# A fused four-layer attention and expert kernel: the scores of two heads are computed together at every second step, the turn of the probabilities stands behind q's product, and the output products at the step's end

## The reference, cut to what matters

```python
x = x + jnp.tanh(g_xattn[0]) * _L0_xattn_ref(_layernorm(x), ctx_2048, ...)   # 16 heads of 128
x = x + jnp.tanh(g_ffn[0])   * _L0_ffn_ref(_layernorm(x), ...)               # 8 experts, the best 2
x = x + jnp.tanh(g_xattn[1]) * _L1_xattn_ref(_layernorm(x), ctx_2048, ctx_2048)
x = x + jnp.tanh(g_ffn[1])   * _L1_ffn_ref(_layernorm(x), ...)               # 8 experts, the best 1
# first layer, for each sequence b and head h:
q = rms_norm(x @ q_w + q_b, nq_s);  k = rms_norm(ctx @ ki_w + ki_b, nki_s);  v = ctx @ vi_w + vi_b
scores = jnp.einsum('bshd,blhd->bhsl', q, k) * scale
attn = softmax(scores);  out = jnp.einsum('bhsl,blhd->bshd', attn, v);  out @ o_w + o_b
```

## Time and profile before

| | |
|---|---|
| median of the runs | 1361.11 us |
| the profiled execution | 1362.31 us, its span 1360.5 us |
| TensorE: matmuls | 1332.2 us busy, 98% |
| TensorE: weight loads | 1170.8 us busy, 86% |
| VectorE / ScalarE | 769.0 us (57%) / 761.0 us (56%) |
| GpSimd | 74.1 us (5%) |
| granted TensorE clock, mean | 0.997 |

### The profile page before, as it was taken

One profiled execution on the slowest core, in us unless ns is written; L12 is line 12 of the kernel. 1 busy time (PEld: TensorE's weight loads), 2 busy tenths in 40 slices (PEclk: granted clock), 3 DMA queues, 4 the chain that ended last, 5 costly groups with the idle time before them and its releaser, 6 DMA issues.

```text
span 1360.5 us, 26830 instructions
## 1 busy us (share of the span) xinstructions
PE 1332.2 (98%) x10479; PEld 1170.8 (86%) x10479; DVE 769.0 (57%) x2323; ACT 761.0 (56%) x2084; POOL 74.1 (5%) x114
## 2 busy tenths in 40 slices
PE   7899999999999999999999999999999999999998
PEld 6788888988898888988889888998889888888877
DVE  7644556546565464664555465564656555554575
ACT  4375666566465564756556564555646556456522
POOL 3000000010000000000000100001000000001010
PEclk9999999999999999999999999999999999999999
DMA  8312522223122321222212231122312112122100
GB/s 300 112 63 78 140 94 74 68 66 121 47 78 64 94 94 47 63 94 83 89 47 77 69 120 63 47 79 92 111 32 78 63 63 94 49 76 72 54 1 32
DMA packets 51452, 108.48 MB, mean 80 GB/s; under 512 B 8224, under 2 KB 32000, under 8 KB 50688
## 3 DMA queue, kind: packets, MB, share of 16 engines
q1 hardware_dynamic: 51328, 106.77, 24.2%
HBM read 89.98 MB, written 16.78 MB: 78 GB/s over the span
## 4 chain that ended last, share of the span: by engine, by line
PE 86%; DVE 10%; ACT 3%; issue 1%; DMA 0%; SPq 0%; DVEq 0%
PE bank L114 57%; PE bank L1044 8%; PE bank L1054 5%; PE bank L1015 3%; PE bank L1033 3%; PE bank L1154 2%; PE bank L1166 2%; PE bank L1191 1%; PE bank L1005 1%; PE bank L1108 1%; ACT xn L783 1%; PE bank L985 1%; DVE rstd L80 1%; DVE logit L1516 1%; DVE ao_lo L1507 1%
## 5 line engine op out<-in xcount | busy, mean ns | idle before, releaser
L114 PE MATMUL bank<-sv,ct_hi 128*128 128x256 f32 x1024 | 195.4, 289 | 0.0
L114 PE MATMUL bank<-so,ao_hi 128*128 128x256 f32 x1016 | 187.6, 284 | 0.3 <-DVE ao_lo L1507 0.3
L1507 DVE SCALAR_TENSOR_TENSOR ao_lo<-bank,vecs,ao_hi 128x512 fp32r<-128x512 f32 x127 | 95.3, 751 | 159.6 <-ACT ao_hi L752 158.4
L758 ACT ACTIVATE expo<-logit,least 128x64 f32<-128x64 f32 x512 | 171.6, 337 | 21.7 <-DVE least L1518 21.7
L752 ACT ACTIVATE ao_hi<-bank,vecs 128x512 fp32r<-128x512 f32 x127 | 87.0, 685 | 154.4 <-PE bank L1044 153.8
L114 PEld LDWEIGHTS bank<-so,ao_hi 128*128 128x128 f32 x1016 | 162.1, 189 | 8.5 <-issue 0.5
L114 PEld LDWEIGHTS bank<-sv,ct_hi 128*128 128x128 f32 x1024 | 156.3, 189 | 0.1
L777 ACT ACTIVATE q_sb<-bank,qbias,qscale 128x512 f32<-128x512 f32 x128 | 99.3, 776 | 87.2 <-PE bank L114 86.7
L1516 DVE TENSOR_TENSOR logit<-bank,rr 128x256 f32<-128x256 f32 x128 | 54.3, 424 | 163.3 <-PE bank L1054 162.7
L114 PE MATMUL bank<-sv,ct_lo 128*128 128x256 f32 x512 | 143.2, 280 | 0.0
L114 PE MATMUL bank<-so,ao_lo 128*128 128x256 f32 x508 | 142.1, 280 | 0.0
(11 more groups left out here) (236 smaller groups left out, 2721.1 us busy)
## 6 DMA issues: line engine op xcount, KB each, us to landing
sv<-v_scratch SPq DMA_DIRECT2D x56, 512.0 KB, 3.4
so<-o_scratch SPq DMA_DIRECT2D x56, 512.0 KB, 3.3
xin<-in_x_dram SPq DMA_DIRECT2D x8, 512.0 KB, 4.9
cin<-in_ctx_dram SPq DMA_DIRECT2D x32, 128.0 KB, 4.9
xres<-in_x_dram SPq DMA_DIRECT2D x8, 512.0 KB, 4.8
c_scratch<-cs SPq DMA_DIRECT2D x8, 512.0 KB, 5.0
v_scratch<-sv SPq DMA_DIRECT2D x8, 512.0 KB, 2.8
o_scratch<-so SPq DMA_DIRECT2D x8, 512.0 KB, 2.6
```

Source lines behind the costliest of these rows:

```text
L114: last = pe.matmul(out, lhs[a], rhs[b], start=start and n == 0, stop=stop and n == 2, **kw)
L758: last = act.activation(expo[:, t, :], logit[:, t, :], ACT.Exp, scale=-1.0, bias=least[:, t:t + 1], accum_out=rsum[:, t:t + 1])
L1507: dve.scalar_tensor_tensor(out=lo[:, :], in0=attention_bank(g, h)[:, :], scalar=vecs[:, v:v + 1], in1=hi[:, :].bitcast(F32), op0=ALU.add, ...
```

## The change

`scores` of two heads, h-2 and h-1, now stand together at every even step, between `attend` and k's product; they fill the two halves of the bank `at_ps`, and `q_sb`, `logit` and `least` get two buffers each. `expo` is gone: the exponentials are written over the logits. `exps` and `probabilities` of a head move from one step behind it to two steps behind it (at even steps the scores were just made, at odd steps they are a step old). `prob_transpose` moves from between k and v to behind q's product. `output` moves from the head of the step to its end, of the head h-3 in place of h-4. So TensorE's order in a step is

```diff
 PREP_BANKS = 6
-TURN_LAG, ATT_LAG, OUT_LAG = 2, 3, 4
+TURN_LAG, ATT_LAG, OUT_LAG = 2, 3, 3
 POINTS = "abcde"
...
     nqk_t = sb("nqk_t", [P, 2 * NT])
-    least = sb("least", [P, NT])
+    least = sb("least", [P, 2, NT])
     rsum = sb("rsum", [P, NT])
...
     k_sb = sb("k_sb", [P, 2, GT])
-    q_sb = sb("q_sb", [P, GT])
-    logit = sb("logit", [P, NT, SEQ])
-    expo = sb("expo", [P, NT, SEQ])
+    q_sb = sb("q_sb", [P, 2, GT])
+    logit = sb("logit", [P, 2, NT, SEQ])
     prob = sb("prob", [P, NT, SEQ])
...
         def exps(g, h):
...
             for t in range(NT):
-                last = act.activation(expo[:, t, :], logit[:, t, :], ACT.Exp, scale=-1.0, bias=least[:, t:t + 1],
+                last = act.activation(logit[:, h % 2, t, :], logit[:, h % 2, t, :], ACT.Exp, scale=-1.0, bias=least[:, h % 2, t:t + 1],
                                       accum_out=rsum[:, t:t + 1])
...
             else:
-                act.activation(q_sb[:, :], bank[:, :], ACT.Identity, scale=qscale[:, h:h + 1],
+                act.activation(q_sb[:, h % 2, :], bank[:, :], ACT.Identity, scale=qscale[:, h:h + 1],
                                bias=qbias[:, h:h + 1]).then_inc(pj_read.sem, 1)
...
         def step(b, h):
-            main = live(b, h)
+            main, final = live(b, h), h == H - 1 and not is_body(b, NG - 1)
             share(b, h, "a")
...
             if live(b, h - TURN_LAG):
-                prob_copy(b, h - TURN_LAG)
-            share(b, h, "c")
-            if live(b, h - 1):
-                exps(b, h - 1)
+                exps(b, h - TURN_LAG)
             if main:
                 project(b, h, 1)
-                if h == H - 1 and not is_body(b, NG - 1):
+                if final:
                     split_context(b + 1)
+            share(b, h, "c")
+            if (b, h) == (LAST, H - 1):
+                project(b, h, 2)
+            if live(b, h - TURN_LAG):
+                prob_copy(b, h - TURN_LAG)
+            if main and (b, h) != (LAST, H - 1):
+                project(b, h, 2)
+                if final:
+                    split_tokens(b + 1)
             share(b, h, "d")
-            if main:
-                project(b, h, 2)
-                if h == H - 1 and not is_body(b, NG - 1):
-                    split_tokens(b + 1)
             share(b, h, "e")
...
             step(LAST, h)
-        exps(LAST, H - 1)
+        exps(LAST, H - 2)
         attn_hi(LAST, H - 3)
         prob_copy(LAST, H - 2)
+        exps(LAST, H - 1)
+        attn_hi(LAST, H - 2)
         expert_exp(NEXT)
-        attn_hi(LAST, H - 2)
         prob_copy(LAST, H - 1)
...
         def scores(g, h):
             pe.wait_ge(pj_read.sem, pj_read.count(g, 3 * h + 2))
-            l_ready.wait(pe, g, h - 1)
+            l_ready.wait(pe, g, h - 1 if (g, h) == (LAST, H - 1) else h - 1 - h % 2)
             for t in range(NT):
...
                     s = slice(t * P + i * SEQ, t * P + (i + 1) * SEQ)
-                    last = pe.matmul(at_ps[i * SEQ:(i + 1) * SEQ, t * SEQ:(t + 1) * SEQ],
-                                     q_sb[:, s], k_sb[:, h % 2, keys(t, i)], start=True, stop=True)
+                    last = pe.matmul(at_ps[i * SEQ:(i + 1) * SEQ, (h % 2 * NT + t) * SEQ:(h % 2 * NT + t + 1) * SEQ],
+                                     q_sb[:, h % 2, s], k_sb[:, h % 2, keys(t, i)], start=True, stop=True)
             last.then_inc(qk_full.sem, 1)
...
         def step(b, h):
             main = live(b, h)
-            if live(b, h - OUT_LAG):
-                output(b, h - OUT_LAG)
             if live(b, h - ATT_LAG):
...
             share(b, h, "a")
+            if (b, h) == (0, 2):
+                gr_read.wait(pe, 0, 2 * NT - 1)
+            if h % 2 == 0 and live(b, h - 2):
+                scores(b, h - 2)
+                scores(b, h - 1)
+            if (b, h) == (LAST, H - 1):
+                scores(b, h - 1)
             if main and (b, h) != (0, 0):
...
             share(b, h, "b")
+            if main:
+                values(b, h)
+            share(b, h, "c")
             if (b, h) == (0, 1):
                 norms(-1)
-                gr_read.wait(pe, 0, 2 * NT - 1)
-            if live(b, h - 1):
-                scores(b, h - 1)
+            if main:
+                project(b, h, 2)
             if live(b, h - TURN_LAG):
                 prob_transpose(b, h - TURN_LAG)
-            share(b, h, "c")
-            if main:
-                values(b, h)
             share(b, h, "d")
-            if main:
-                project(b, h, 2)
+            if (b, h) == (LAST, H - 1):
+                scores(b, h)
+            if live(b, h - OUT_LAG):
+                output(b, h - OUT_LAG)
             share(b, h, "e")
...
         def end():
-            for t in range(NT):
+            for t in range(1, NT):
                 expert_rows(NEXT, t)
...
             step(LAST, h)
-        scores(LAST, H - 1)
-        output(LAST, H - 4)
         attend(LAST, H - 3)
...
         attend(LAST, H - 2)
+        output(LAST, H - 3)
         prob_transpose(LAST, H - 1)
-        output(LAST, H - 3)
+        output(LAST, H - 2)
         attend(LAST, H - 1)
-        output(LAST, H - 2)
+        expert_rows(NEXT, 0)
         output(LAST, H - 1)
...
         def logits(g, h):
 
-            dve.wait_ge(qk_full.sem, qk_full.count(g, h))
+            dve.wait_ge(qk_full.sem, qk_full.count(g, h if (g, h) == (LAST, H - 2) else h + 1 - h % 2))
             if h == 0:
                 dve.wait_ge(rr_ready.sem, rr_ready.count(g, 0))
-            chain.link(dve.tensor_tensor(logit[:, :, :], at_ps[:, 0:NT * SEQ].rearrange("p (t l) -> p t l", t=NT),
-                                         rr[:, (g - (h < 0)) % 2, :, :], ALU.mult))
-            dve.tensor_reduce(least[:, :], logit[:, :, :], AXX, ALU.min).then_inc(l_ready.sem, 1)
+            u = h % 2
+            chain.link(dve.tensor_tensor(logit[:, u, :, :], at_ps[:, u * NT * SEQ:(u + 1) * NT * SEQ].rearrange(
+                "p (t l) -> p t l", t=NT), rr[:, (g - (h < 0)) % 2, :, :], ALU.mult))
+            dve.tensor_reduce(least[:, u, :], logit[:, u, :, :], AXX, ALU.min).then_inc(l_ready.sem, 1)
 
         def probabilities(g, h):
...
             chain.link(dve.reciprocal(rinv[:, :], rsum[:, :]))
-            dve.tensor_tensor(prob[:, :, :], expo[:, :, :], rinv[:, :].unsqueeze(2).to_broadcast([P, NT, SEQ]),
+            dve.tensor_tensor(prob[:, :, :], logit[:, h % 2, :, :], rinv[:, :].unsqueeze(2).to_broadcast([P, NT, SEQ]),
                               ALU.mult).then_inc(p_ready.sem, 1)
...
         def step(b, h):
...
                 split(b, 0)
-            if live(b, h - TURN_LAG):
-                probabilities(b, h - TURN_LAG)
-            if h == 0 and not is_body(b, 0) and live(b, 0):
                 split(b, 1)
...
                 attn_lo(b, h - ATT_LAG)
-            if is_body(b, 0) and h == 1:
+            if (b, h) == (0, 1):
                 score_factors(0)
-            if live(b, h - 1):
+            if h % 2 == 0 and live(b, h - 2):
+                logits(b, h - 2)
                 logits(b, h - 1)
+            if (b, h) == (LAST, H - 1):
+                logits(b, h - 1)
+            share(b, h, "b")
+            if live(b, h - TURN_LAG):
+                probabilities(b, h - TURN_LAG)
+            share(b, h, "c")
             if live(b, h - TURN_LAG):
                 prob_copy(b, h - TURN_LAG)
-            share(b, h, "b")
-            share(b, h, "c")
             share(b, h, "d")
...
         logits(LAST, H - 1)
+        attn_lo(LAST, H - 3)
+        prob_copy(LAST, H - 2)
         for j in range(2):
             expert_logits(NEXT, j)
+        attn_lo(LAST, H - 2)
+        probabilities(LAST, H - 1)
+        prob_copy(LAST, H - 1)
         expert_choice(NEXT)
-        prob_copy(LAST, H - 2)
-        attn_lo(LAST, H - 3)
-        probabilities(LAST, H - 1)
-        attn_lo(LAST, H - 2)
-        prob_copy(LAST, H - 1)
         expert_scale(NEXT)
...
         end()

```

## The result

The changed kernel takes 1370.17 us (median of four runs, 1369.37 to 1371.67) against 1361.52 for the kernel before in the same comparison: ratio 1.0062, 95% interval 1.0047 to 1.0077. So it is slower by some 8.5 us. The forecast was 1377.0 with slower at .67; the measured time lies in its range, and the size was taken almost twice too large.

A forecast was written before the change was run, and what follows sets the result against it. TensorE, busy 98% of the span, was taken as the bound. Terms summed to +15.9 us on the profiled 1362.31, so 1378.2; the median of runs is 1.2 lower: 1377.0, range 1351 to 1387.

The forecast's parts named there:

- pair, 62 times: TensorE's scores and turns: two heads cost 1.76 us in place of 2.00, .24 a pair, -15.1 us for 62 pairs.
- affinity and attention broken up: At (11,b), (12,b) and the second attention at (13,b) the neighbour is gone: 3 x .21 x 7 groups, +4.4 us.
- waits that go: TensorE's waits for `ao_lo` ahead of the turn (1.7 us) and for `sums` ahead of the gram products (2.0) go: -3.7.
- start: The 3.03 us wait at the start goes, with a few products at half clock behind it: -4 us.
- turn waits: plain, steps 0, 11, 12, 14 of group 7: Turn waits for exponentials behind k's copy: chain 2.94 against TensorE's 2.82; th copies delay steps 11 and 12; together +12.3 us.
- step 6: ScalarE normalises before splitting the attention, so the turn waits 1.0 us with restart in 7 groups: +7.0 us.
- step 8: Choice of experts starts late, so the turn waits .7 us in six groups and 1.9 in group 7: +6.1 us.
- step 14: VectorE's eight factors stand ahead of the copy, so `attend` of step 15 waits .9 us in 6 groups: +5.4 us.
- tail: Choice of experts stands ahead of the last `attend`, some 2.2 us, plus 1.3 for one output less in reserve: +3.5.
- The estimate of .33 from the Trainium skill: Two drains of about 166 ns saved a pair: .33 us, 20.6 in all, sum 1371.6; the forecast stayed with the rows.
- The rival by which a way out stands between the two heads: Pairing saves nothing: a pair costs 1.32 + .22, gain .02 a pair, +13.6 us, 1390.6; chance .05.
- The faster rival: Queues feeding the turn keep up; steps 6, 8, 14 and plain ones cost nothing: -9.6 us, 1351.5; chance .24.

The follow-up runs named there:

- the repaired kernel: Changed kernel with edits to normalisation, score factors (except group 0), tail order, exponentials of steps 11 and 12, (12,b) affinity and choice's exponential together: 1353.13 us, ratio .9935.

## Why the prediction was right, and where it was off

The direction and its reason held: pairs gain, and late queues at the turn take more than that. Term by term, measured by the distances of `attend` and of q's last product to the turn (.07 added to each wait, see below; the second and the third row are worked out from the distances inside the steps, good to about .5):

| term | forecast | measured |
|---|---|---|
| pair, 62 times | -15.1 | -13.6 (.22 each) |
| affinity and attention broken up | +4.4 | +4.7 |
| waits that go | -3.7 | -8.1 |
| start | -4 | -3.15 |
| turn waits: plain, steps 0, 11, 12, 14 of group 7 | +12.3 | +13.1 |
| step 6 | +7.0 | +6.2 |
| step 8 | +6.1 | +3.2 |
| step 14 | +5.4 | +3.0 |
| tail | +3.5 | +4.9 |
| sum | +15.9 | +10.3 |

The span says +9.4, so the rows don't close. No row, forecast or measured, has what groups 0 and 7 have alone: in group 0 step 14, 2.5 below a plain even step (the wait of 1.62 and the half clock behind it are gone), step 3, 1.6 above a plain odd one (half clock), and waits of `attend` of .87 and .63 ahead of steps 12 and 0; in group 7 step 10, .6 beside its turn. With the rows they would give about 11; the other -1.7 is scattered over the steps, a few hundredths in each. That omissions of 1 to 2.5 us of both signs come out so small is luck.

**Pair.** Right in sum (its -15.1 is .24 for 63 pairs; 62 give -14.9). The forecast took pair and move as one, and the run with unpaired scores took them apart: .35 from pairing, -.13 from the new place. The estimate of .33 from the Trainium skill ("TensorEngine Tiling (Array Packing)", Key Properties, with the drain from "TensorE: Matmul & The Clock Gate", Single matmul latency) agrees with the .35 of pairing alone. That it is a drain no run shows, and the affinity's change of shape costs .20 for both ends, so .33 is not the price of every change. The forecast set it against the sum of pairing and move, where the rows gave the better number. The rival by which a way out stands between the two heads falls: a second head adds 1.28 - .81 = .47, its stream.

**Waits that go.** The failing step was to take the recorded idle time as the wait. The gram products' wait stood as .29 in the row, but from v's first product to the gram it took 1.94 and now takes 1.48, .46; ahead of the turn in step 6 scores took .95 in place of .61, .34 for a row of .27; and in step 3 v took 1.69 for 1.41 with no idle in any row. The forecast also left out the turn's own wait for the probabilities in step 15: scores there took .83 and the turn had .14 of idle ahead of it, .21 by the distance. Some 1.3 a group in place of .55; step 10 has it in seven groups, the others in six.

**Plain steps.** The chain of 2.94 against 2.82 was right to a few hundredths: where it rules, in steps 2 and 15, the wait is .14, .21 with the .07 (forecast .18 with the restart). But it rules two steps a group, not four; the others have work at b or c that covers it. Instead group 1 and group 0 have the .14 in a dozen other turns. These are plain steps too, since the shares that stand there from group 2 on are missing: in step 3 of group 1 v's first product stands .23 behind k's last, and q's first 1.40 behind v's, as in step 2 of group 4; in step 3 of group 2 it is 1.63 and 1.76. In all, 18 of the 28 forecast turns have it in groups 1 to 7, and 8 in group 0, which the forecast did not count; that the row comes out near is in part luck. Steps 11 and 12, forecast .38, cost .39: the best hit of the whole sum, and shown by the run that takes only them away.

**Steps 6, 8 and 14.** The mechanisms are shown by a run each (normalisation, choice's exponential, factors). The sizes were too large where two logits follow each other: the forecast charged 1.82, they take 1.57 (.79 a head for .91). The way of TensorE was right: 8.9 in step 14, forecast 8.9. The chains were too long. From turn to turn step 8 takes 10.6 against 11.1, and in step 14 the factors start 6.5 behind `attend` against 7.0: .25 of that is the logits, the other .25 was not traced. So in step 8 a wait of .7 became .27, in step 14 .9 became .51. The forecast's own step 8 has a slip as well: 11.1 less 10.3 is .8 and 11.1 less 9.1 is 2.0, where it takes .7 and 1.9. A wait is the small difference of two long chains; an error of 5% in a chain of 10 us is half of it.

**Start.** The wait of 3.03 went, as forecast. The half clock did not go in this execution: it moved behind the new waits of 1.22 and .72, where it costs 1.36 in step 3 of group 0, outside this row.

**Tail.** Right in place, low by 1.4. One thing was left out: `prob_copy` of head 14 behind `attn_lo` of head 13, the 1.85 in the tail rows, which the run with the tail's new order takes to .82. The half clock behind that wait is .9 of the tail's 4.9.

**The faster rival** (the queues keep up, 1351.5) fell with the change as written, and is what the repaired kernel does: 1353.1. The change's idea was good for 9 us, and its schedule gave 17 away.

What stays open: why the granted clock falls behind the same wait in one execution and not in another, and where the other .25 in the chains of steps 8 and 14 lies.

## What to carry to other kernels

Moving a small product next to its like saves the change of shape twice (.35 us for scores, .20 for the affinity), but whatever is moved takes its producers' deadlines along: for each queue that feeds the moved piece, write the chain from the last common event to its new place, and look at each step in which a share stands in that chain. Cheap repairs are found there: in all five edits that gained it was enough to let the piece that TensorE waits for go ahead of one that can wait. Compare steps by the distance between equal instructions, not by recorded idle time; read the granted clock of a stretch before its time is put down to an edit (here it moved single distances by .9 to 1.4 us); and check the first group of a table-driven schedule apart, since other readers may wait there.

## What was not expected of the hardware

A wait of TensorE costs more than its idle time in the record: a turn with .15 recorded as idle (step 11) cost .39 in the step.

The same wait is not followed by the same clock. Ahead of the last `attend` but one, eight of the kernels with the tail as changed wait 1.85. In six of their profiled executions the granted clock fell to .50 there; in two (the exponentials ahead of k's copy, the choice's exponential) it stayed at 1.00. Ten of the kernels have the waits of 1.2 and .7 to .8 at the start; the clock fell there in seven of the executions and stayed at 1.00 in three.

The smallest waits at the turn are all alike, .36 to .37 between q's last product and the turn where .23 is the least. That is one chain and no smallest wait of the hardware: in the changed kernel all 26 such turns stand 3.16 or 3.17 behind k's last product.
